# First layer's scan: GpSimd reads and writes the image in row order in the column directions, and VectorE and ScalarE do the reordering

## The reference

```python
z = silu(depthwise3x3(in_w @ norm(x)))                 # (4, 96, 64, 64), L = 4096
x0 = z.reshape(B, 96, L)                               # row by row
x1 = swapaxes(z, 2, 3).reshape(B, 96, L)               # column by column
xs = stack([x0, x1, flip(x0), flip(x1)], axis=1)       # 4 directions
dts_r, Bs, Cs = split(einsum('bkdl,ked->bkel', xs, x_proj_weight))
delta = softplus(einsum('bkrl,kdr->bkdl', dts_r, dt_w) + dt_bias)
dA = exp(delta * A);  dBu = delta * Bs * xs
h[l] = dA[l] * h[l-1] + dBu[l]                         # scan over 4096 places
y = h * Cs + Ds * xs
ym = y0 + y1 (turned back) + y2 (flipped) + y3 (flipped, turned back)
```

## Time and profile before

| | us |
|---|---|
| median of 3 runs | 1581.51 (1580.91 to 1585.74) |
| profiled execution, its own time | 1586.61 |
| its span | 1584.7 |
| busy in the span: PE, DVE, ACT, POOL | 1235.0, 1220.5, 1110.7, 905.2 |
| first layer's scan within the span | about 222 to 477 |

### The profile page before, as it was taken

The page is one execution under the profiler, slowest core; times in us unless marked ns, Lnnn a source line. Parts: engine busy times, 40 slices in busy tenths (PEclk is TensorE's granted clock), DMA queues, the critical chain, the costliest instruction groups (busy, mean ns, idle before and its releaser), DMA issues. The chain is left out here.

```text
span 1584.7 us, 14386 instructions
## 1 busy us (share of the span) xinstructions
PE 1235.0 (78%) x3822; PEld 436.1 (28%) x3822; DVE 1220.5 (77%) x1226; ACT 1110.7 (70%) x1643; POOL 905.2 (57%) x451
## 2 busy tenths in 40 slices
PE   3899935656554777777898998989989898776995
PEld 2344301111102555422222222222222221112663
DVE  1655638989882777505999999999999999993775
ACT  2677366767642777668888888988889888631664
POOL 2400049999993333227788777887778877750000
PEclk8999955555556999876988789887898978555997
DMA  5444390201002333229777877778777887615572
GB/s 147 118 141 121 98 184 24 106 0 48 6 40 73 95 99 88 75 75 213 183 167 173 191 178 170 171 173 190 174 177 168 177 186 164 147 37 129 121 177 58
DMA packets 136428, 200.53 MB, mean 127 GB/s; under 512 B 26739, under 2 KB 68770, under 8 KB 135564
## 3 DMA queue, kind: packets, MB, share of 16 engines
q1 hardware_dynamic: 133740, 196.15, 51.1%
q10 hardware_dynamic: 2160, 2.61, 0.6%
q0 software_dynamic: 448, 0.85, 0.2%
HBM read 145.93 MB, written 53.63 MB: 126 GB/s over the span
## 5 line engine op out<-in xcount | busy, mean ns | idle before, releaser
L1349 POOL TENSOR_TENSOR m_ub<-m_dlb,m_bt 128x1536 f32<-128x1536 f32 x128 | 440.4, 3442 | 145.7 <-DVE m_h L1703 139.7
L1703 DVE TENSOR_TENSOR_SCAN m_h<-m_qa,m_state,m_ub 128x512 f32<-128x512 f32 x384 | 463.7, 1261 | 53.3 <-POOL m_ub L1349 51.7
L1665 ACT ACTIVATE m_qa<-m_dlb,k_a 128x512 f32<-128x512 f32 x384 | 255.2, 685 | 109.5 <-DVE m_h L1703 104.0
L1714 DVE TENSOR_TENSOR m_g<-m_h,m_qc 128x1536 f32<-128x1536 f32 x128 | 221.7, 1732 | 18.4 <-issue 12.5
L1532 PE MATMUL m_qc<-m_bcr,k_selc 32*128 32x512 f32 x256 | 167.8, 739 | 83.0 <-DVE m_g L1714 82.7
L1074 POOL TENSOR_TENSOR b_u<-b_dl,b_z 128x1024 f32<-128x1024 f32 x48 | 124.4, 2594 | 155.9 <-DMA b_z<-scratch_z 151.5
L1549 PE MATMUL m_qy<-m_g,k_seld 128*32 128x512 f32 x768 | 168.4, 739 | 0.0
L939 PE MATMUL b_qb<-b_bc,k_pack_sel 96*128 96x512 bf16 x96 | 58.9, 613 | 100.7 <-DVE b_u L1021 92.4
L1085 POOL TENSOR_TENSOR b_y<-b_y,b_g 128x1024 f32<-128x1024 f32 x48 | 129.7, 2703 | 3.9 <-DVE b_g L1043 3.9
L1473 PE MATMUL m_qf<-m_cva,k_conv 113*96 113x504 f32 (+1 forms) x192 | 126.0, 808 | 5.0 <-PEq L1105 5.0
L1532 PEld LDWEIGHTS m_qc<-m_bcr,k_selc 32*128 32x128 f32 x256 | 42.9, 209 | 208.4 <-issue 190.0
(11 more groups left out here) (178 smaller groups left out, 2286.5 us busy)
## 6 DMA issues: line engine op xcount, KB each, us to landing
m_dlb<-scratch_dldu SPq DMA_DIRECT2D x128, 384.0 KB, 9.7
m_bt<-scratch_brow SPq DMA_DIRECT2D x128, 256.0 KB, 5.9
scratch_dldu<-m_dldu SPq DMA_DIRECT2D x32, 384.0 KB, 4.9
scratch_z<-a_z SPq DMA_DIRECT2D x24, 256.0 KB, 6.0
b_z<-scratch_z SPq DMA_DIRECT2D x3, 2048.0 KB, 11.8
scratch_y<-b_y SPq DMA_DIRECT2D x12, 512.0 KB, 2.6
c_y<-scratch_y SPq DMA_DIRECT2D x16, 384.0 KB, 3.4
scratch_gate<-m_gt SPq DMA_DIRECT2D x32, 192.0 KB, 4.8
```

The lines of the kernel that those rows point to most:

```text
L1349: nc.gpsimd.tensor_tensor(ub[k % 3][:], dlb[u % 2][:, J:2 * J, :], bcast(bt[u % 2][:, n, :], J), ALU.mult).then_inc(ub_ready, 1)
L1665: nc.scalar.activation(q_a[:, j, :], dlb[u % 2][:, j, :], ACT.Exp, scale=G["a1"][:, j, n:n + 1]).then_inc(da, 1)
L1703: nc.vector.tensor_tensor_scan(h[k % 3][:, j, :], q_a[:, j, :], ub[k % 3][:, j, :], state[:, k % NS, j:j + 1], ALU.mult, ALU.add).then_inc ...
L1714: nc.vector.tensor_tensor(g[k % 2][:], h[k % 3][:], bcast(q_c[:], J), ALU.mult).then_inc(read, 1)
```

## The change

In column directions `dl`, `u` and `g` are now kept in row order, and only `h`, `b_qa` and a new tile `ub` are in column order. The softplus writes `dl` in row order, in runs of 8 elements. `decay` reads `dl` with 16 elements from one to the next. GpSimd's two operations go through `z` and `y` in row order, in runs of 16 elements, and through `dl`, `u` and `g` from end to end. `drive` reads `u` with 16 elements from one to the next and writes `ub` in column order; `times_c` writes `g` with 16 elements from one to the next. In row directions the order of elements stays as it was, but `drive` writes `ub` there too. With `ub` a tile of its own, `drive` has a further wait, for the scan of step i - 2, which read `ub`; and GpSimd's product waits for `drive` of step i - 2 in place of its scan.

```diff
-        u, h, g = ([m.sb(f"b_{n}{s}", [P, TC]) for s in range(2)] for n in ("u", "h", "g"))
+        u, ub, h, g = ([m.sb(f"b_{n}{s}", [P, TC]) for s in range(2)] for n in ("u", "ub", "h", "g"))
...
-        def from_rows(ap, col):
-            return ap.rearrange("p (h w) -> p w h", h=H) if col else ap
+        def from_rows(ap, col, v=None):
+            if not col:
+                return ap if v is None else ap[:, v * CH:v * CH + CH]
+            ap = ap.rearrange("p (h w) -> p w h", h=H)
+            return ap if v is None else ap[:, v * (CH // H):(v + 1) * (CH // H), :]
+        def image(tile, col, piece):
+            if not col:
+                return tile[:, piece * TC:piece * TC + TC]
+            return tile.rearrange("p (h w) -> p h w", h=H)[:, :, piece * TC // H:(piece + 1) * TC // H]
+        def half_rows(ap, col, v):
+            if not col:
+                return ap[:, v * CH:v * CH + CH]
+            return ap.rearrange("p (h w) -> p h w", h=H)[:, :, v * (CH // H):(v + 1) * (CH // H)]
...
-                    nc.scalar.activation(by_column(dl[s][:, part], col), from_rows(q_dt[:, part], col), ACT.Softplus).then_inc(delta, 1)
+                    nc.scalar.activation(half_rows(dl[s][:], col, v), in_rows(q_dt[:, part], col), ACT.Softplus).then_inc(delta, 1)
...
-                nc.scalar.activation(q_a[i % 2][:], dl[i % DL][:], ACT.Exp, scale=a0[:, j, k:k + 1]).then_inc(da_ready, 1)
+                nc.scalar.activation(by_column(q_a[i % 2][:], col), from_rows(dl[i % DL][:], col), ACT.Exp, scale=a0[:, j, k:k + 1]).then_inc(da_ready, 1)
...
-                half_u = by_column(u[s][:, part], col)
-                nc.vector.tensor_tensor(half_u, half_u, from_rows(q_b[:], col), ALU.mult).then_inc(driven, 1)
+                dve.wait_ge(scanned, freed(i))
+                nc.vector.tensor_tensor(by_column(ub[s][:, part], col), from_rows(u[s][:], col, v), from_rows(q_b[:], col), ALU.mult).then_inc(driven, 1)
...
-                nc.vector.tensor_tensor_scan(h[s][:, way], q_a[s][:, way], u[s][:, way], carried,
+                nc.vector.tensor_tensor_scan(h[s][:, way], q_a[s][:, way], ub[s][:, way], carried,
...
-                nc.vector.tensor_tensor(by_column(g[s][:, part], col), by_column(h[s][:, part], col), from_rows(q_c[:], col),
+                nc.vector.tensor_tensor(from_rows(g[s][:], col, v), by_column(h[s][:, part], col), from_rows(q_c[:], col),
...
-                    pool.wait_ge(scanned, freed(i))
-                    nc.gpsimd.tensor_tensor(by_column(u[s][:], col), by_column(dl[i % DL][:], col),
-                                            seen(z[j % 2][:], col, piece), ALU.mult).then_inc(u_ready, 1)
+                    pool.wait_ge(driven, half(i - 2, 1))
+                    nc.gpsimd.tensor_tensor(in_rows(u[s][:], col), in_rows(dl[i % DL][:], col),
+                                            image(z[j % 2][:], col, piece), ALU.mult).then_inc(u_ready, 1)
...
-                    part = seen(y[j % 2][:], col, piece)
-                    nc.gpsimd.tensor_tensor(part, part, by_column(g[i % 2][:], col), ALU.add).then_inc(added, 1)
+                    part = image(y[j % 2][:], col, piece)
+                    nc.gpsimd.tensor_tensor(part, part, in_rows(g[i % 2][:], col), ALU.add).then_inc(added, 1)
```

More of the change, by code:

```diff
@@ L973, in delta_of @@
                     act.wait_ge(dt_mm, half(i, v))
-                    nc.scalar.activation(by_column(dl[s][:, part], col), from_rows(q_dt[:, part], col), ACT.Softplus).then_inc(delta, 1)
+                    nc.scalar.activation(half_rows(dl[s][:], col, v), in_rows(q_dt[:, part], col), ACT.Softplus).then_inc(delta, 1)
             def decay(i):
-                j, k = i // n, steps[i % n][0]
+                j, k, col = i // n, steps[i % n][0], steps[i % n][1]
                 act.wait_ge(delta, half(i, 1))
                 act.wait_ge(scanned, freed(i))
-                nc.scalar.activation(q_a[i % 2][:], dl[i % DL][:], ACT.Exp, scale=a0[:, j, k:k + 1]).then_inc(da_ready, 1)
+                nc.scalar.activation(by_column(q_a[i % 2][:], col), from_rows(dl[i % DL][:], col), ACT.Exp, scale=a0[:, j, k:k + 1]).then_inc(da_ready, 1)
             def begin_y(j, c):
```

## The result

The changed kernel takes 1588.89 us (median of 8 runs, 1585.91 to 1591.32), the one before 1581.93 (8 runs, 1576.88 to 1585.74). The ratio is 1.0043 with a 95% interval of 1.0028 to 1.0058: about 7 us slower. The forecast was 29.8 us slower. The time lies in its range and on its side, but the loss is a quarter of the one forecast.

A forecast was written before the change was run, and what follows sets the result against it. GpSimd was taken to bound the scan's column steps. VectorE's stepped accesses add 44.9 us, less 15.1 of GpSimd's lateness: +29.8 on 1581.5 gives 1611.3 us, range 1577 to 1634.

The forecast's parts named there:

- What bounds the kernel before: Scan's column steps: GpSimd sets them at 5.8 us against VectorE's 4.89; a faster GpSimd can give 15.1 us.
- GpSimd at 4.6 us a step: GpSimd's product and sum in column steps: runs of 16 neighbours taken as costing nothing, 4.6 us, at worst 6.1.
- The fourth rival: GpSimd's runs of 16 cost as much as long steps, staying at 5.8 us a step; no chance beyond a shared 0.07.
- I take one slot, 0.53: VectorE's drive and times_c in column steps: each stepped operation of 512 elements takes 0.53 us more.
- d: Added time of one VectorE drive (512 elements, stepped read of u) in column steps; forecast 0.53 us.
- w: Added time of one VectorE times_c (512 elements, stepped write of g) in column steps; forecast 0.53 us.
- the prediction's sum: VectorE's column step, start to start: 6.76 us, 1.87 over 4.89; 44.9 us in 24 steps, less 15.1, is +29.8.
- GpSimd's slow pace: At 2.3 ns an element, GpSimd can hide part of a slow read; VectorE, at 1.03 ns, has nothing to hide it.
- GpSimd's rows: GpSimd's stepped-access prices scaled to 512 elements on VectorE: d = 0.25, w = 0.11 us.
- The second rival: VectorE pays no more than GpSimd for stepped access: 5.50 us a column step, about 0 change, 1581 us; chance 0.07.
- The turning point at d + w = 0.44: Where VectorE's added time in 24 column steps equals the 15.1 us gain; below it the kernel is faster.
- the first case: VectorE pays over half a slot per stepped element and becomes the bound: +4 to +50 us; chance 0.78.

The follow-up runs named there:

- Run 2: Changed kernel with drive's read of u and times_c's write of g undone to end to end in column directions (computation altered): 0.989, 1564.8 us.
- run 5: Changed kernel with VectorE's drive and times_c stepping through pairs of neighbours in column directions (computation altered): 0.9907 to the kernel before, 1566.8 us.
- 7: Whole change with dl, u and g in row order by pairs of rows (h / 2, w, h mod 2), computation correct: 0.9894 to the kernel before, 1564.6 us.
- Runs 1: Changed kernel with only ScalarE's decay undone, reading dl end to end in column directions (computation altered): 1.0046 to the kernel before, 1589.7 us.
- Run 4: Changed kernel with u and g at 24 or 17 places per row of 16 elements: 1.0281, 1625.9 us for 24; 1.0070, 1591.2 us for 17.
- product_only: Half of the change: dl, u, GpSimd's product and decay in row order, g and the sum into y as in the kernel before: 1.0007.
- sum_only: Half of the change: g and the sum into y in row order, dl, u, product and decay as in the kernel before: 0.9987.

## Why the prediction was right in direction and wrong in size

- **What bounds the kernel before: right.** GpSimd's total set the scan, worth 15.1 us. Run 2 gained 1581.55 - 1564.78 = 16.8 us, and runs 5 and 7 gained 16 and 17. The 15.1 are a net figure. GpSimd's column pace, 5.83 us, stood 0.94 over VectorE's 4.89, which is 22.6 us in 24 steps, but it began the column steps with a lead (in the second group the first two pass at 4.84 and 4.89 us from scan to scan, the fourth to seventh at 5.83 to 5.88) and made part of its lateness good in the shorter row steps (4.6 us). So the 8 column steps of that group took 350.92 - 307.14 = 43.8 us, 5.5 each. In the changed kernel VectorE has no such slack, and they take 45.9. That is how a pace of 5.79 us on VectorE is dearer than one of 5.83 on GpSimd.
- **GpSimd at 4.6 us a step, its runs of 16 for nothing: right** (2.34 us, and waits for VectorE in 44 places). The fourth rival is out.
- **VectorE the new bound, the rest covered: right.** Runs 1 and 2 show it from both sides. The new wait of `drive` cost nothing on the path: in row steps 0.16 us of issue stand where 0.17 for TensorE stood, and the step stays at 4.89.
- **The term that was mis-sized: "I take one slot, 0.53".** Measured, `drive` pays 0.33 us in duration (0.32 from start to start) and `times_c` 0.33 in duration but 0.25 to 0.27 from start to start: the next instruction starts 0.85 to 0.87 after it, against 0.60. With d = 0.32 and w = 0.27, the prediction's sum gives 24 x (2 x 0.59 - 0.25) - 15.1 = +7.2, where 7.0 was measured between the medians and 6.6 between the scans. So the sum was sound and one number in it was 1.8 times too large. The argument for it failed as well: GpSimd's slow pace was said to hide most of a dearer access. Per element GpSimd pays 0.50 / 1024 = 0.49 ns for its stepped read and VectorE 0.33 / 512 = 0.64. They differ by a third, not by a factor of two. GpSimd's rows (d = 0.25, w = 0.11) were too low for both, but nearer: they give d + w = 0.36, the forecast 1.06, and 0.59 was measured. The second rival, built on them and given 0.07, ended 8 us from the measured time, the forecast 22.
- **The turning point at d + w = 0.44** made the result touchy: the loss is a small difference between 21.6 and 15.1, and 0.1 us in each operation is 9.6 us. The direction came out for the reason given, but by a margin of 0.15 in d + w where the forecast had 0.62, and near the lower end of the first case (+4 us).
- **The Trainium skill's Vector Engine (DVE) Microarchitecture Reference, section on measured stream behaviour on trn2, spoke against the change: right, and set aside too lightly.** Its 1.73 and 1.71 ns, for far hops, gave +12 us; the trace has 1.03 + 0.64 = 1.67 ns for a step of 16 words. I kept away from them since they were for larger steps, with 2.50 for 24 words as the nearer case. Run 4 shows that the dearer value does belong to 24 words, and not to 16 or 17.
- **ScalarE's decay: the size was guessed well** (0.89 us, 1.05 forecast), and its cover held. The row used for a free step, 216 against 213 ns for 12 elements, had nothing to say: at 0.87 ns an element it would have shown 10 ns, too little to read from four instructions of 206 to 222.

## What to carry to other kernels

Work taken off the engine that sets the pace is worth only the lateness it causes, here 15.1 us and not the 29 us by which GpSimd's instructions shrank; set against this what the next engine pays, step by step. When a layout must be turned somewhere, look first for one in which every access meets two neighbouring 4-byte words: here that turned a loss of 7 us into a gain of 17 with the same instructions. If half of a change is tried alone, look at loops through another engine's single buffer, which the other half may have hidden.

## What the runs showed of the hardware

- VectorE, float32, one SBUF operand of 512 elements whose elements stand alone: 64 bytes apart 1.0 us, 68 bytes 1.05, 96 bytes 1.4; in pairs, or whole, 0.68. I hadn't expected 96 bytes to cost twice what 64 do.
- The same price falls on a stepped read (`drive` alone, run `product_only`: 0.99 to 1.02 us) and on a stepped write (`times_c` alone, run `sum_only`: 1.02), but from start to start the write shows 0.25 to 0.27 of its 0.33 us.
- ScalarE pays 0.85 to 0.89 us for 1024 elements read from SBUF one by one (`decay` with a step of 16: 2.01 us against 1.12; the copy of z with a step of 64: 1.98 against the 1.13 of `begin_y`), and at most 0.13 in pairs (1.13 to 1.25 us).
- PSUM read in steps of 8 elements costs VectorE at most 14 ns in 687 and ScalarE's softplus nothing (594 ns); VectorE in pairs (run 5) stays at 674 to 680 ns.
- GpSimd reads and writes in steps of 2 float32 elements at 2.40 to 2.44 us against 2.34 to 2.36, where steps of 64 took 2.84 and 3.06.
